# Graph attention kernel: the 0/1 matrix of destinations and the edge weights move into PSUM, and the two halves of a fetched set are masked by one VectorE operation

## The chip, the cores and the metric

The kernel runs on one core of one Trainium2 chip. The metric is the device time of one execution in microseconds (us). The engines are TensorE (PE, with its weight loads PEld), VectorE (DVE), ScalarE (ACT), GpSimd (POOL) and SyncE (SP, which here only issues transfers).

## What is computed

A graph attention layer with 4 heads is followed by a mixture of 16 experts, both on 6250 nodes with 256 features; the graph has 200,000 edges, sorted by destination. Cut to the graph part:

```
h_fwd, h_rev = h @ W_forward.T, h @ W_reverse.T          # 64 features each
messages = h_fwd[src] * direction[:, 0:1] + h_rev[src] * direction[:, 1:2]
scores = leaky_relu(einsum('ef,hf->eh', messages, attn_forward[0]), 0.2)
exp_scores = exp(scores - scores.max(axis=0))
norm = exp_scores / (segment_sum(exp_scores, dst, N)[dst] + 1e-10)
out = stack([segment_sum(messages * norm[:, hd:hd+1], dst, N) for hd in range(H)], axis=1)
```

The expert part (layer norm, gate, top 2 of 16 experts, two products each, layer norm) comes after it and is not touched by the change.

## The kernel before

A first stage makes a node table in DRAM. Each of its rows holds, for one node, 68 numbers of the forward weights (64 features and 4 score parts) and 68 of the reverse weights: 136 numbers. The edge stage, `stage_edges` from line 779 on, then goes through the edges in 98 chunks of 2048: 128 partitions by K = 16 sets of 128 edges. Two chunks are in the ring at a time (slots s = 0 and 1). The later stages (nodes, experts, final norm) take the last quarter of the time.

For one chunk c the work is:

- **GpSimd** (line 899) issues one indirect DMA per set (`gather`, line 262), which fetches the table rows of 128 source nodes into `rows`. The node numbers are offsets that the instruction reads from the tile `index` in SBUF. 14 of the 16 sets come this way; the last four chunks and the first two differ a little. Between the gathers stand waits on VectorE's messages (`msg_ready`), scores (`score_ready`) and TensorE's sums (`summed`) of the chunks before.
- **TensorE** (line 939) makes the other two sets (FILL = 2) by products instead of a fetch: `fetch` (line 959) multiplies a 0/1 matrix `onehot` by the table held in SBUF (`parts`), 28 products of 476 columns into `p_hot`, for 7 candidate places and for the two halves of the row (d = 0 and 1), each half in a PSUM bank of its own. It also sums the chunk's weighted messages into windows of nodes (line 878, `p_win`).
- **VectorE** (line 987) waits for all 16 sets, multiplies the rows by the edges' two weights (lines 990, 994 and 997, where the weights are read from `index` in SBUF), makes the 0/1 matrix `hot` of destinations (line 1003), adds the score parts (1009), applies the leaky part (1011), keeps the maximum (1016), adds the windows of the chunk before into the sums (985), adds forward and reverse parts into `msg` (1023), multiplies `hot` by the exponentials `ex` into `hot_ex` (1027), and, in `keep` (line 1049), masks the two fetched sets by place (1054, one operation for each half) and reduces them over the 7 places (1059). `build_hot` (1044) makes the next `onehot`.
- **ScalarE** takes the exponential (928), and **SyncE** loads `index` and `key` for the chunk after next (lines 888 and 892).

The order on each engine is the order in which the program is written; engines wait for each other by counting semaphores. The PSUM bank `p_dve` is VectorE's own and already holds `iota_p`, `rev_p` and `group_p`; the sum `p_part` is in PSUM too. All other operands of the lines above are in SBUF.

```
dve.tensor_tensor(rows[:, s, :, 0:COLS], rows[:, s, :, 0:COLS],
                  attr_of[:, 0, :].unsqueeze(2).broadcast_to([P, K, COLS]), ALU.mult)
```

Of the kernel before, what the change touches and what calls it, by code (L numbers as in the profile page):

```python
# [18 lines left out]
F32 = mybir.dt.float32  # L19
BF16 = mybir.dt.bfloat16  # L20
# [199 lines left out]
def stage_edges(nc, tensors, g):  # L220
# [4 lines left out]
    with ExitStack() as edges:  # L225
# [9 lines left out]
        before = esb("before", [1, NCH], I32)  # L235
        behind = esb("behind", [P, NU])
        place = esb("place_of_source", [P, NF])
        place_no = esb("place_no", [P, PLACES])
        key = esb("key", [P, RING, FILL, P])
        onehot = esb("onehot", [P, FILL, GP, P], F32R)  # L240
        group_first = esb("group_first", [P, GP])
# [25 lines left out]
        with ExitStack() as ctx:  # L267
# [128 lines left out]
            @block.gpsimd  # L396
            def _(pool):
                pool.memset(ident[:, :], 0.0).then_inc(s_init, 1)
                pool.wait_ge(s_init, 1)
                pool.affine_select(out=ident[:, :], in_=ident[:, :], compare_op=ALU.not_equal, fill=1.0,  # L400
                                   base=0, pattern=[[-1, P]], channel_multiplier=1).then_inc(s_ident, 1)
                pool.memset(ones[:, :], 1.0).then_inc(s_ident, 1)
                pool.iota(iota_w[:, :], pattern=[[1, W]], base=0, channel_multiplier=0,
                          allow_small_or_imprecise_dtypes=True).then_inc(s_ident, 1)
                pool.iota(place_no[:, :], pattern=[[GP * P, PLACES]], base=0, channel_multiplier=0,
                          allow_small_or_imprecise_dtypes=True).then_inc(s_ident, 1)
                pool.iota(group_first[:, :], pattern=[[P, GP]], base=0, channel_multiplier=1,
                          allow_small_or_imprecise_dtypes=True).then_inc(s_ident, 1)
                pool.memset(g["shared"][0:MSG, x_at + NT * D:HEADS * (NP + W)], 0.0).then_inc(s_init, 1)
                pool.wait_ge(s_hot, 32)  # L410
                def clear_x(i):

                    for copies, n in copied_part(i):
                        pool.wait_ge(copies, n)
                    pool.memset(x_rows[0:MSG, PARTS[i]:PARTS[i + 1], :], 0.0).then_inc(x_zeroed, 1)

                source = hot_key[0:NF // 3, :, :]
                late = hot_late[0:NF // 3, 0, :, :]
                rest, step = (spare[:, 6 * P + m * NF:6 * P + (m + 1) * NF] for m in range(2))
                pool.tensor_copy(source, source.bitcast(I32)).then_inc(s_init, 1)  # L420
                pool.tensor_copy(rest, place[:, :].bitcast(I32)).then_inc(s_init, 1)
                n = 4
                pool.wait_ge(s_init, n)
                pool.tensor_copy(place[:, :], rest).then_inc(s_init, 1)
                for much in (4, 2, 1):
                    for of, by in ((source, late), (rest, step)):
                        pool.tensor_scalar(by, of, float(much * GP * P), float(much * GP * P), ALU.is_ge, ALU.mult)\
                            .then_inc(s_init, 1)
                    n += 2 + (much == 4)
                    pool.wait_ge(s_init, n)  # L430
                    for of, by in ((source, late), (rest, step)):
                        pool.tensor_tensor(of, of, by, ALU.subtract).then_inc(s_init, 1)
                    n += 2
                    pool.wait_ge(s_init, n)
                pool.tensor_tensor(place[:, :], place[:, :], rest, ALU.subtract).then_inc(s_init, 1)
                assert n + 1 == KEYED

                for i in range(LATE):
                    pool.wait_ge(s_part, i + 1)
                    pool.tensor_tensor(part_of_parts(i, 1), tab[:, i % 4, 0:PARTS[i + 1] - PARTS[i], :],  # L440
                                       part_of_parts(i, 0).bitcast(F32), ALU.subtract).then_inc(s_init, 1)
                    clear_x(i)
                for i in range(LATE, NPART):
                    clear_x(i)

                for v in range(4):
                    pool.wait_ge(s_stored[v], 16 * ((NPART + 3 - v) // 4))
                pool.wait_ge(s_max, 2 * NPART)
                pool.wait_ge(s_init, parts_done)
                pool.wait_ge(s_low, low_late)  # L450
                for s in range(RING):
                    pool.wait_ge(index_ready[s], 16)
                    gather(pool, s, range(KG, K), early_rows)
                for s in range(EARLY + 1):
                    gather(pool, s, range(KG if s < EARLY else EARLY_SETS), gathered[s])
# [323 lines left out]
        with ExitStack() as ctx:  # L779
            sb, ps, sem = tensors(ctx)  # L780
            msg = sb("msg", [P, K, MSG])
            hot = sb("hot", [P, K, W], BF16)
            hot_ex = sb("hot_ex", [P, K, HEADS, W])
            raw = sb("raw", [P, K, HEADS])
            score = sb("score", [P, K, HEADS])
# [1 line left out]
            iota_x = sb("iota_x", [P, W])  # L787
            p_part = ps("p_part", [P, K, HD])
            p_win = ps("p_win", [P, 512])
            p_hot = ps("p_hot", [P, FILL, 2, 512])  # L790
            ex = sb("ex", [P, K, HEADS])
            p_dve = ps("p_dve", [P, 512])
            iota_p = p_dve[:, 0:W]
            rev_p = p_dve[:, W:W + K * HEADS].rearrange("p (k h) -> p k h", k=K)
            group_p = p_dve[:, W + K * HEADS:W + K * HEADS + GP]
            p_x = p_dve[:, 512 - HEADS * W:512]

            turns = sem("pool_turns")
            rev_part = sem("reverse_part_ready")
            fwd_part = sem("forward_part_ready")  # L800
            rev_score = sem("reverse_scores_ready")
# [42 lines left out]
            def all_rows(eng, c, s, it):  # L844

                eng.wait_ge(gathered[s], arrived(c, it))
                if isinstance(it, int) and it == 0:
                    eng.wait_ge(early_rows, 16 * HOT)
                elif not whole(it):
                    eng.wait_ge(hot_kept, 2 * (fill_of(s, it) + FILL))  # L850
# [32 lines left out]
            @block.sync  # L883
            def _(sp):
                def step(c, s, it, _):
                    if not whole(it):
                        sp.wait_ge(hot_built, FILL * (c - 1))
                        sp.dma_start(key[:, s, :, :], keys[ds(c * FILL, FILL), :].partition_broadcast(P))\
                          .then_inc(key_ready[s], 16)
                    after(sp, gathered[s], 16 * KG * it)  # L890
                    sp.wait_ge(rev_score, c - RING + 1)
                    sp.dma_start(index[:, s, :, :], edge[c] if isinstance(c, int)
                                 else edge[ds(c, 1)].rearrange("a p m k -> (a p) m k")).then_inc(index_ready[s], 16)

                sp.wait_ge(early_rows, 16 * HOT)
                chunks(sp, lambda it: None, step, RING)
# [38 lines left out]
            def _(pe):  # L935
# [23 lines left out]
                def fetch(f, s, it, j):  # L959

                    after(pe, hot_kept, 2 * (f - FILL + 1))
                    pe.wait_ge(hot_built, HOT + f + 1)
                    for gr in range(GP):
                        for m in range(2):
                            for d in range(2):
                                last = pe.matmul(p_hot[:, j, d, 0:PLACES * COLS], onehot[:, j, gr, :],  # L966
                                                 parts[:, gr:NT:GP, m, d * COLS:(d + 1) * COLS],
                                                 start=(gr == 0 and m == 0), stop=(gr == GP - 1 and m == 1))
                    last.then_inc(hot_rows, 1)
# [5 lines left out]
            def _(dve):  # L975
# [9 lines left out]
                    return dve.tensor_tensor(to, to, psum.rearrange("p (h w) -> p h w", h=HEADS), ALU.add)  # L985

                def step(c, s, it, loaded):
                    all_rows(dve, c, s, it)
                    attr_of = index[:, s, 1:3, :].bitcast(F32)
                    dve.tensor_tensor(rows[:, s, :, 0:COLS], rows[:, s, :, 0:COLS],  # L990
                                      attr_of[:, 0, :].unsqueeze(2).broadcast_to([P, K, COLS]), ALU.mult)\
                       .then_inc(fwd_part, 1)
# [56 lines left out]
                def keep(f, s, it, j):  # L1049

                    dve.wait_ge(hot_rows, f + 1)
                    found = p_hot[:, j, :, 0:PLACES * COLS].rearrange("p d (v c) -> p d v c", v=PLACES)
                    for d in range(2):
                        last = dve.scalar_tensor_tensor(  # L1054
                            out=found[:, d], in0=place_no[:, :].unsqueeze(2).broadcast_to([P, PLACES, COLS]),
                            scalar=place[:, ds(f, 1)], in1=found[:, d], op0=ALU.is_equal, op1=ALU.mult)
                    last.then_inc(hot_kept, 1)
                    dve.wait_ge(hot_kept, 2 * f + 1)
                    dve.tensor_reduce(rows[:, s, KG + j, :].rearrange("p (d c) -> p d c", d=2),  # L1059
                                      found.rearrange("p d v c -> p d c v"), AX.X, ALU.add).then_inc(hot_kept, 1)  # L1060

                def finish(c):

# [1133 lines left out]
```

## Time and profile before

| | |
|---|---|
| median of 3 runs | 2537.11 us (2532.44 to 2537.75) |
| the profiled execution, its own time | 2544.06 us |
| its span | 2542.3 us |
| POOL, PE, PEld, DVE, ACT busy | 67%, 79%, 69%, 73%, 14% |
| edge stage, first to last gather | about 62 to 1881 us of the span |

The profile is of one execution, on the only core. A busy share is an average over stages; which engine sets the pace of the edge stage has to be read from who waits for whom there. The time of a group of instructions can hold time in which the instruction stood still, if the engine had started it: a mean that lies above the shortest ones is a sign of that. "Idle before" is what an engine spent before a group, with what ended that time.

### The profile page before, as it was taken

What the parts mean: (1) busy time and instruction counts of PE and PEld (TensorE: products, weight loads), DVE (VectorE), ACT (ScalarE), POOL (GpSimd) and SP (SyncE); (2) the same over time, 40 slices, a digit from 0 to 9 for tenths busy, and PEclk for the clock granted to TensorE, in tenths of its full rate; (3) what the DMA queues carried; (4) which work ended last, traced back from release to release, by engine and by line L of the source; (5) the groups of instructions that cost most, each with busy time, mean ns of one, the idle gap of its engine ahead of it and who ended that gap; (6) DMA issues with size and microseconds to landing.
All of it is one profiled execution on the core that took longest, in us unless ns stands there. A gap on an engine that the chain in (4) does not pass through costs nothing.

```text
span 2542.3 us, 44100 instructions
## 1 busy us (share of the span) xinstructions
PE 2020.8 (79%) x11977; PEld 1765.1 (69%) x11978; DVE 1854.4 (73%) x4481; ACT 349.5 (14%) x936; POOL 1709.5 (67%) x1757
## 2 busy tenths in 40 slices
PE   7688888887888888788888888888727579999970
PEld 6577777676777777667777777777626568888870
DVE  6777777877777787777778777777747866666657
ACT  4100000000000000000000000000015524444435
POOL 6777777777777777777777777777745753333327
PEclk9699999999999899999999999999955589999995
DMA  6222222222222222222222222222244676655657
GB/s 203 61 63 59 64 59 64 61 59 63 59 64 58 63 61 59 63 59 64 58 64 61 59 64 59 64 58 64 57 135 131 211 228 199 196 196 197 198 167 270
DMA packets 176304, 256.65 MB, mean 101 GB/s; under 512 B 47078, under 2 KB 120999, under 8 KB 176004
## 3 DMA queue, kind: packets, MB, share of 16 engines
q0 software_dynamic: 53696, 121.60, 19.5%
q1 hardware_dynamic: 122564, 134.56, 17.3%
q8 instruction: 16, 0.26, 0.0%
q14 instruction: 28, 0.23, 0.0%
HBM read 218.11 MB, written 38.79 MB: 101 GB/s over the span
## 4 chain that ended last, share of the span: by engine, by line
POOL 42%; issue 25%; DVE 15%; PE 6%; DVEq 5%; DMA 5%; ACT 1%; SPq 0%; POOLq 0%; ACTq 0%
POOL rows L262 42%; DVEq L1704 3%; DMA rows<-node_table,index 2%; PE p_y L1872 1%; DVE p_y L1927 1%; PE p_h L1862 1%; DVE shared L985 1%; PE p_win L878 1%; DVE second L1907 1%; DVE hid_t L1899 1%; DVE p_part L994 1%; DVE back L1912 1%; DMA out<-shared 1%; DVE msg L1023 1%; DMA shared<-in_x 1%
## 5 line engine op out<-in xcount | busy, mean ns | idle before, releaser
L262 POOL DMA_INDIRECT rows<-node_table,index x1375 | 1378.3, 1002 | 443.8 <-issue 423.7
L966 PE MATMUL p_hot<-parts,onehot 128*128 128x476 f32 x5264 | 1193.4, 387 | 9.4 <-DVE rows L1059 5.1
L966 PEld LDWEIGHTS p_hot<-parts,onehot 128*128 128x128 f32 x5264 | 1003.7, 192 | 169.7 <-issue 14.4
L878 PE MATMUL p_win<-hot_ex,msg 128*65 128x64 f32 x3136 | 282.3, 268 | 334.4 <-DVE hot_ex L1027 333.3
L878 PEld LDWEIGHTS p_win<-hot_ex,msg 128*65 128x65 f32 x3136 | 267.5, 182 | 372.4 <-issue 372.4
L990 DVE TENSOR_TENSOR rows<-rows,index 128x1088 f32<-128x1088 f32 x98 | 126.7, 1292 | 333.0 <-DMA rows<-node_table,index 332.0
L1713 POOL DMA_INDIRECT expert_rows<-ys,back x104 | 103.0, 990 | 270.9 <-DVE ys L1932 199.0
L928 ACT ACTIVATE ex<-score,neg_shift 128x64 f32<-128x64 f32 x98 | 34.2, 349 | 1758.0 <-DVE score L1011 1758.0
L1054 DVE SCALAR_TENSOR_TENSOR p_hot<-place_no,place_of_source,p_hot 128x476 f32<-128x476 f32 x376 | 249.9, 709 | 0.0
L985 DVE TENSOR_TENSOR shared<-shared,p_win 65x64 f32 x784 | 170.3, 217 | 97.0 <-PE p_win L878 4.0
L1059 DVE TENSOR_REDUCE rows<-p_hot 128x136 f32<-128x952 f32 x188 | 216.1, 1150 | 6.5
L1862 PEld LDWEIGHTS p_h<-xt,shared 128*128 128x128 f32 x1664 | 199.9, 194 | 30.2 <-ACT xt L1804 27.5
L1862 PE MATMUL p_h<-xt,shared 128*128 128x128 f32 x1664 | 211.9, 281 | 7.2 <-ACT xt L1804 7.1
L1044 DVE TENSOR_TENSOR onehot<-key,p_dve 128x896 fp32r<-128x896 f32 x188 | 202.9, 1079 | 0.0
L1872 PE MATMUL p_y<-shared,hid_t 128*128 x832 | 198.7, 382 | 2.6 <-DVE hid_t L1899 2.2
L1872 PEld LDWEIGHTS p_y<-shared,hid_t 128*128 128x128 f32 x832 | 151.1, 192 | 19.7 <-issue 3.2
L1899 DVE TENSOR_SCALAR hid_t<-p_h,shared 128x128 f32<-128x128 f32 x208 | 63.4, 346 | 118.7 <-PE p_y L1872 79.5
L1283 POOL DMA_INDIRECT dispatched<-xn,slot_i x98 | 99.9, 1019 | 57.7 <-issue 35.2
L994 DVE TENSOR_TENSOR p_part<-rows,index 128x1024 f32<-128x1024 f32 x98 | 120.1, 1226 | 0.0
L1027 DVE TENSOR_TENSOR hot_ex<-hot,ex 128x1024 f32<-128x1024 bf16 x98 | 119.1, 1215 | 0.0
L1023 DVE TENSOR_TENSOR msg<-rows,p_part 128x1024 f32<-128x1024 f32 x98 | 118.5, 1209 | 0.0
L1835 ACT ACTIVATE own<-xs,is_first 128x256 f32<-128x256 f32 x104 | 52.9, 508 | 199.4 <-DVE is_first L1910 199.3
(268 smaller groups left out, 1408.2 us busy)
## 6 DMA issues: line engine op xcount, KB each, us to landing
shared<-in_w SPq DMA_DIRECT2D x120, 512.0 KB, 4.5
rows<-node_table,index POOLq DMA_INDIRECT x1375, 2.8
xs<-dispatched SPq DMA_DIRECT2D x104, 129.5 KB, 4.1
key<-hot_keys SPq DMA_DIRECT2D x94, 128.0 KB, 3.0
shared<-expert_rows SPq DMA_DIRECT2D x12, 896.0 KB, 7.8
token_rows<-in_x SPq DMA_DIRECT2D x7, 896.0 KB, 13.1
shared<-in_x SPq DMA_DIRECT2D x7, 768.0 KB, 9.0
out<-shared SPq DMA_DIRECT2D x6, 896.0 KB, 7.5
```

The costliest lines, as they stand in the source:

```text
L262: pool.indirect_dma_start(out=rows[:, s, k, :], out_offset=None, in_=table, in_offset=bass.IndirectOffsetOnAxis(ap=index[:, s, 0, k:k + 1] ...
L878: last = pe.matmul(psum[0:MSG, u * HEADS * W:(u + 1) * HEADS * W], msg[:, k, :], weighted[:, k, :, :].rearrange("p h w -> p (h w)"), start ...
L966: last = pe.matmul(p_hot[:, j, d, 0:PLACES * COLS], onehot[:, j, gr, :], parts[:, gr:NT:GP, m, d * COLS:(d + 1) * COLS], start=(gr == 0 an ...
L985: return dve.tensor_tensor(to, to, psum.rearrange("p (h w) -> p h w", h=HEADS), ALU.add)
L990: dve.tensor_tensor(rows[:, s, :, 0:COLS], rows[:, s, :, 0:COLS], attr_of[:, 0, :].unsqueeze(2).broadcast_to([P, K, COLS]), ALU.mult)\
L994: dve.tensor_tensor(p_part[:, :, :], rows[:, s, :, COLS:COLS + HD], attr_of[:, 1, :].unsqueeze(2).broadcast_to([P, K, HD]), ALU.mult)\
L1023: dve.tensor_tensor(msg[:, :, 0:HD], rows[:, s, :, 0:HD], p_part[:, :, :], ALU.add)\
L1044: dve.tensor_tensor(onehot[:, j, :, :], key[:, s, j, :].unsqueeze(1).broadcast_to([P, GP, P]), group_p.unsqueeze(2).broadcast_to([P, GP, P ...
L1054: last = dve.scalar_tensor_tensor(out=found[:, d], in0=place_no[:, :].unsqueeze(2).broadcast_to([P, PLACES, COLS]), scalar=place[:, ds(f, ...
L1059: dve.tensor_reduce(rows[:, s, KG + j, :].rearrange("p (d c) -> p d c", d=2), found.rearrange("p d v c -> p d c v"), AX.X, ALU.add).then_i ...
L1862: last = pe.matmul(p_h[:, u, f // 2, (f % 2) * P:(f % 2 + 1) * P], w1_r[:, r % R5, c, f * P:(f + 1) * P], xt[:, u, c, :], start=(c == 0), ...
L1872: last = pe.matmul(p_y[:, u, 0:D], hid_t[:, u, c, :], w2_sb[:, ds(e, 1), c, :] .rearrange("p a d -> p (a d)"), start=(c == 0), stop=(c == ...
```

## The change

`hot` becomes part of the PSUM bank `p_dve`, in 32-bit floats and no longer bfloat16 in SBUF. A new VectorE copy brings the chunk's edge weights (128 x 32) from `index` into the same bank as `weight_p`, ahead of the wait for the gathered rows, and lines 990, 994 and 997 read them there. SyncE's load of `index` now waits for that copy and no longer for the reverse scores. In `p_hot` the two halves of a fetched set now end and begin at the border of two banks, so that they adjoin, and `place_no` is written twice over, so that one operation masks both.

```diff
-        place_no = esb("place_no", [P, PLACES])
+        place_no = esb("place_no", [P, 2 * PLACES])
...
-                pool.iota(place_no[:, :], pattern=[[GP * P, PLACES]], base=0, channel_multiplier=0,
+                pool.iota(place_no[:, :], pattern=[[0, 2], [GP * P, PLACES]], base=0, channel_multiplier=0,
...
-            hot = sb("hot", [P, K, W], BF16)
...
-            p_hot = ps("p_hot", [P, FILL, 2, 512])
+            p_hot = ps("p_hot", [P, FILL, 1024])
+            half = PLACES * COLS
+            hot_from = 512 - half
...
+            hot_at = W + K * HEADS + GP
+            weight_at = hot_at + K * W
+            assert weight_at + 2 * K <= 512 - HEADS * W
+            weight_p = p_dve[:, weight_at:weight_at + 2 * K].rearrange("p (d k) -> p d k", d=2)
+            hot = p_dve[:, hot_at:hot_at + K * W].rearrange("p (k w) -> p k w", k=K)
...
-                    sp.wait_ge(rev_score, c - RING + 1)
+                    sp.wait_ge(weights_copied, c - RING + 1)
                     sp.dma_start(index[:, s, :, :], edge[c] if isinstance(c, int)
...
-                                last = pe.matmul(p_hot[:, j, d, 0:PLACES * COLS], onehot[:, j, gr, :],
+                                last = pe.matmul(p_hot[:, j, hot_from + d * half:hot_from + (d + 1) * half], onehot[:, j, gr, :],
...
                 def step(c, s, it, loaded):
+                    dve.wait_ge(index_ready[s], 16 * (it + 1))
+                    after(dve, raw_ready, c)
+                    after(dve, rev_part, c)
+                    dve.tensor_copy(weight_p, index[:, s, 1:3, :].bitcast(F32)).then_inc(weights_copied, 1)
                     all_rows(dve, c, s, it)
-                    attr_of = index[:, s, 1:3, :].bitcast(F32)
+                    dve.wait_ge(weights_copied, c + 1)
+                    attr_of = weight_p
...
-                    found = p_hot[:, j, :, 0:PLACES * COLS].rearrange("p d (v c) -> p d v c", v=PLACES)
-                    for d in range(2):
-                        last = dve.scalar_tensor_tensor(
-                            out=found[:, d], in0=place_no[:, :].unsqueeze(2).broadcast_to([P, PLACES, COLS]),
-                            scalar=place[:, ds(f, 1)], in1=found[:, d], op0=ALU.is_equal, op1=ALU.mult)
-                    last.then_inc(hot_kept, 1)
+                    found = p_hot[:, j, hot_from:hot_from + 2 * half]
+                    both = found.rearrange("p (v c) -> p v c", c=COLS)
+                    dve.scalar_tensor_tensor(
+                        out=both, in0=place_no[:, :].unsqueeze(2).broadcast_to([P, 2 * PLACES, COLS]),
+                        scalar=place[:, ds(f, 1)], in1=both, op0=ALU.is_equal, op1=ALU.mult).then_inc(hot_kept, 1)
```

The two places where VectorE's order changes are in the body of the loop over chunks. The first is the start of a chunk. Before:

```order
L850 ISA [waits gathered0]
L990 TENSOR_TENSOR rows<-rows,index 128x16x68 [waits one_hot_rows_kept]
L994 TENSOR_TENSOR p_part<-rows,index 128x1024 [waits messages_ready]
L997 TENSOR_TENSOR p_dve<-rows,index 128x64
L1003 ISA [waits weighted_hot_ready]
L1003 TENSOR_TENSOR hot<-dst_rel,p_dve 128x256
```

And with the change (its lines are numbered by the new file: 1002, 1006, 1009 and 1015 are the old 990, 994, 997 and 1003):

```order
L998 COPY p_dve<-index 128x32 [waits reverse_part_ready,raw_scores_ready,index_ready0]
L853 ISA
L857 ISA [waits gathered0]
L1000 REGISTER_ALU [waits one_hot_rows_kept]
L1002 TENSOR_TENSOR rows<-rows,p_dve 128x16x68 [waits edge_weights_in_psum]
L1006 TENSOR_TENSOR p_part<-rows,p_dve 128x1024 [waits messages_ready]
L1009 TENSOR_TENSOR p_dve<-rows,p_dve 128x64
L1015 ISA [waits weighted_hot_ready]
L1015 TENSOR_TENSOR p_dve<-dst_rel,p_dve 128x256
```

One copy is added ahead of the wait for the gathers, and each operation keeps its place; what was read from `index` and written to `hot` now lies in `p_dve`. The second place is `keep`, on VectorE at the end of the chunk. Before:

```order
L1054 SCALAR_TENSOR_TENSOR p_hot<-place_no,place_of_source,p_hot 128x476 [waits one_hot_rows_summed]
L1054 SCALAR_TENSOR_TENSOR p_hot<-place_no,place_of_source,p_hot 128x476
L1059 TENSOR_REDUCE rows<-p_hot 128x136 [waits one_hot_rows_kept]
L1054 SCALAR_TENSOR_TENSOR p_hot<-place_no,place_of_source,p_hot 128x476 [waits one_hot_rows_summed]
L1054 SCALAR_TENSOR_TENSOR p_hot<-place_no,place_of_source,p_hot 128x476
```

And with the change:

```order
L1066 SCALAR_TENSOR_TENSOR p_hot<-place_no,place_of_source,p_hot 128x952 [waits one_hot_rows_summed]
L1070 TENSOR_REDUCE rows<-p_hot 128x136 [waits one_hot_rows_kept]
L1066 SCALAR_TENSOR_TENSOR p_hot<-place_no,place_of_source,p_hot 128x952 [waits one_hot_rows_summed]
L1070 TENSOR_REDUCE rows<-p_hot 128x136 [waits one_hot_rows_kept]
L1056 TENSOR_TENSOR onehot<-key,p_dve 128x896 [waits one_hot_rows_summed,keys_loaded1]
```

Two operations of 476 elements become one of 952, twice per chunk. GpSimd's and TensorE's instructions keep their number and order.

## Rows read from the trace of the kernel before

**Rows 1.** The page: span, and busy time of each engine.

```profile
span 2542.3 us, 44100 instructions
PE 2020.8 (79%) x11977; PEld 1765.1 (69%) x11978; DVE 1854.4 (73%) x4481; ACT 349.5 (14%) x936; POOL 1709.5 (67%) x1757
```

**Rows 2.** The page: the chain that ended last, shares by engine.

```profile
POOL 42%; issue 25%; DVE 15%; PE 6%; DVEq 5%; DMA 5%; ACT 1%; SPq 0%; POOLq 0%; ACTq 0%
```

**Rows 3.** The view of waits, 300 to 1700 us: total us, times, longest us.

```profile
POOL rows L262 <- issue: 325.2, 1006, 2.2
...
DVE rows L990 <- DMA rows<-node_table,index: 245.8, 76, 5.5
PE p_win L878 <- DVE hot_ex L1027: 228.6, 76, 6.0
```

**Rows 4.** Starts of chunks 3 and 93 on VectorE, from the timeline (start us, duration us).

```profile
142.27 1.29 DVE L990 TENSOR_TENSOR rows<-rows,index 128x1088 f32<-128x1088 f32 x1 [2.91 <-DMA rows<-node_table,index]
...
1809.56 1.29 DVE L990 TENSOR_TENSOR rows<-rows,index 128x1088 f32<-128x1088 f32 x1 [2.92 <-DMA rows<-node_table,index]
```

**Rows 5.** The page's groups: busy us, mean ns of one | idle before, its releaser.

```profile
L262 POOL DMA_INDIRECT rows<-node_table,index x1375 | 1378.3, 1002 | 443.8 <-issue 423.7
...
L990 DVE TENSOR_TENSOR rows<-rows,index 128x1088 f32<-128x1088 f32 x98 | 126.7, 1292 | 333.0 <-DMA rows<-node_table,index 332.0
...
L1054 DVE SCALAR_TENSOR_TENSOR p_hot<-place_no,place_of_source,p_hot 128x476 f32<-128x476 f32 x376 | 249.9, 709 | 0.0
...
L1044 DVE TENSOR_TENSOR onehot<-key,p_dve 128x896 fp32r<-128x896 f32 x188 | 202.9, 1079 | 0.0
...
L994 DVE TENSOR_TENSOR p_part<-rows,index 128x1024 f32<-128x1024 f32 x98 | 120.1, 1226 | 0.0
L1027 DVE TENSOR_TENSOR hot_ex<-hot,ex 128x1024 f32<-128x1024 bf16 x98 | 119.1, 1215 | 0.0
L1023 DVE TENSOR_TENSOR msg<-rows,p_part 128x1024 f32<-128x1024 f32 x98 | 118.5, 1209 | 0.0
```

**Rows 6.** Groups of instructions, 1855.6 to 1871.6 us only: the gathers.

```profile
L262 POOL DMA_INDIRECT rows<-node_table,index x13 | 12.3, 944 | 4.0 <-issue 4.0
```

**Rows 7.** The timeline, one chunk around 1010 to 1023 us, GpSimd and VectorE.

```profile
1010.68 0.95 POOL L262 DMA_INDIRECT rows<-node_table,index  x1 [0.30 <-issue]
...
1013.45 1.29 DVE L990 TENSOR_TENSOR rows<-rows,index 128x1088 f32<-128x1088 f32 x1 [3.04 <-DMA rows<-node_table,index]
1014.43 1.13 POOL L262 DMA_INDIRECT rows<-node_table,index  x1 [0.30 <-issue]
...
1016.51 0.22 DVE L1011 SCALAR_TENSOR_TENSOR score<-raw 128x64 f32<-128x64 f32 x1
...
1016.77 0.23 DVE L1016 TENSOR_TENSOR run_max<-run_max,score 128x64 f32<-128x64 f32 x1
...
1020.57 1.21 DVE L1023 TENSOR_TENSOR msg<-rows,p_part 128x1024 f32<-128x1024 f32 x1
1020.87 0.94 POOL L262 DMA_INDIRECT rows<-node_table,index  x1 [0.30 <-issue]
1021.70 1.22 DVE L1027 TENSOR_TENSOR hot_ex<-hot,ex 128x1024 f32<-128x1024 bf16 x1
1022.12 1.61 POOL L262 DMA_INDIRECT rows<-node_table,index  x1 [0.30 <-DVE msg L1023]
```

**Rows 8.** The timeline: first and last of 97 gathers begun inside L1027.

```profile
95.73 1.22 DVE L1027 TENSOR_TENSOR hot_ex<-hot,ex 128x1024 f32<-128x1024 bf16 x1
96.32 1.44 POOL L262 DMA_INDIRECT rows<-node_table,index  x1 [0.30 <-issue]
...
1880.14 1.21 POOL L262 DMA_INDIRECT rows<-node_table,index  x1 [0.30 <-issue]
```

**Rows 9.** The timeline: a VectorE copy from SBUF into PSUM, and a pair of masks.

```profile
88.89 0.18 DVE L1105 COPY p_dve<-iota_w 128x16 f32<-128x16 f32 x1
...
1004.48 1.33 DVE L1054 SCALAR_TENSOR_TENSOR p_hot<-place_no,place_of_source,p_hot 128x476 f32<-128x476 f32 x2
```

More of the change, by code:

```diff
@@ L796, in stage_edges @@
             p_x = p_dve[:, 512 - HEADS * W:512]
+            hot_at = W + K * HEADS + GP
[3 more added lines that the diff above has]
+            hot = p_dve[:, hot_at:hot_at + K * W].rearrange("p (k w) -> p k w", k=K)
             turns = sem("pool_turns")
+            weights_copied = sem("edge_weights_in_psum")
             rev_part = sem("reverse_part_ready")
@@ L1051, in keep @@
                     dve.wait_ge(hot_rows, f + 1)
-                    found = p_hot[:, j, :, 0:PLACES * COLS].rearrange("p d (v c) -> p d v c", v=PLACES)
-                    for d in range(2):
-                        last = dve.scalar_tensor_tensor(
-                            out=found[:, d], in0=place_no[:, :].unsqueeze(2).broadcast_to([P, PLACES, COLS]),
-                            scalar=place[:, ds(f, 1)], in1=found[:, d], op0=ALU.is_equal, op1=ALU.mult)
-                    last.then_inc(hot_kept, 1)
+                    found = p_hot[:, j, hot_from:hot_from + 2 * half]
[3 more added lines that the diff above has]
+                        scalar=place[:, ds(f, 1)], in1=both, op0=ALU.is_equal, op1=ALU.mult).then_inc(hot_kept, 1)
                     dve.wait_ge(hot_kept, 2 * f + 1)
                     dve.tensor_reduce(rows[:, s, KG + j, :].rearrange("p (d c) -> p d c", d=2),
-                                      found.rearrange("p d v c -> p d c v"), AX.X, ALU.add).then_inc(hot_kept, 1)
+                                      found.rearrange("p (d v c) -> p d c v", d=2, v=PLACES), AX.X, ALU.add).then_inc(hot_kept, 1)
                 def finish(c):
```

## The prediction, made before the changed kernel ran

> **What bounds the kernel now.** I read the page's totals first and then asked who waits. TensorE has the largest busy share [rows 1], but the chain that ended last lies mostly on GpSimd and in "issue" [rows 2]. In the 1400 us from the middle of the edge stage, VectorE stands idle 245.8 us before L990, once per chunk, until a gather's transfer has landed, and TensorE 228.6 us before L878, once per chunk, until VectorE's L1027 is done [rows 3]. That is 3.2 and 3.0 us per chunk of slack on both. GpSimd waits for nobody: its 0.30 us between two gathers is nearly the same everywhere and stands as "issue" [rows 5, 7]. So GpSimd's row of gathers sets the pace, VectorE follows it by a transfer's latency (the last gather of a chunk ends at 1011.63, L990 starts at 1013.45), TensorE follows VectorE. Every eighth chunk one gap of GpSimd is 2.2 us long, also "issue" [rows 3]; nothing in the change touches it, and I leave it. A chunk takes (1809.56 - 142.27) / 90 = 18.53 us [rows 4]. Whatever shortens a gather shortens the time; whatever shortens VectorE alone only adds to its 3 us.
>
> **Gathers are not all alike.** Where VectorE does nothing, a gather takes 944 ns (13 of them) [rows 6]. The mean of all 1375 is 1002 ns [rows 5]. The difference, 1378.3 - 1375 x 0.944 = 80.3 us, is time in which gathers stood still. The timeline shows where [rows 7]: the gather that begins at 1022.12, 0.42 us into L1027, takes 1.61 us; the one that begins at 1014.43, inside L990, takes 1.13; the one that begins at 1020.87, inside L1023, takes 0.94. L990, L994, L997 and L1027 have both inputs in SBUF; L1023 has one in SBUF and one in PSUM. Each long gather is longer by what is left of the VectorE operation less 0.13 us: L1027 ends at 1022.92, 0.80 after the gather's start, and 0.80 - 0.13 is the 0.67 that 1.61 has over 0.94.
>
> - *Weights in PSUM.* L990, L994 and L997 keep one input in SBUF. Their gathers should take 944 ns: -9.7 - 7.3 - 1.8 = -18.8 us.
> - *`hot` in PSUM.* L1027 keeps only `ex` in SBUF: -60.8 us. Both terms lie on GpSimd's row, which is the path, so they count in full.
> - *Operations with a PSUM input.* Does one cost VectorE more? L1023 (one input in PSUM) takes 1209 ns for 1024 elements, L994 and L1027 (none) 1226 and 1215 [rows 5]. I take 0. L1003 writes 32-bit elements into PSUM where it wrote 16-bit ones into SBUF; L994 writes 1024 such in 1226 ns, so again 0.
> - *The new copy.* 128 x 32 into PSUM; the copy of 128 x 16 took 0.18 us [rows 9], so about 0.2 us, from below 0.18, from above 0.23 (L1016, with two inputs of 64) [rows 7]. It stands ahead of the wait for the gathers, where VectorE is idle 3.2 us per chunk [rows 3], so 0 on the path. Its own waits are for the same engine's operations of the chunk before and for an index load made a chunk earlier, all over by then. If the cover were gone it would cost 98 x 0.2 = 20 us.
> - *One mask for two.* Two operations of 476 take 709 ns each, overlap a little, and are done after 1.33 us [rows 5, 9]. At L1044's and L1023's slope, (1209 - 1079) / 128 = 1.02 ns per element, one of 952 takes 709 + 476 x 1.02 = 1.19 us against 1.33 for the pair [rows 5, 9]. It gives VectorE 0.14 us, 0.28 per chunk, which pays for the copy; bounds 0 and 0.24. On the path it is 0, since VectorE waits in any case. That the operation runs across a bank border no row shows; at worst it is the pair's 1.33.
> - *SyncE's queue.* The index load can now go when the gathers of its slot have landed, sooner by L990 and L994, 2.5 us [rows 5], and by L997. It is needed a chunk later: 0.
> - *TensorE.* The same products into the same banks at another column: 0. Its slack goes from 3.0 to 2.2 us per chunk as the period shrinks by 0.8; it stays covered.
> - *What is late next.* VectorE's idle time goes from 3.2 to about 2.4 us per chunk, so GpSimd still leads. Two operations keep two SBUF inputs, L1011 and L1016, 0.22 and 0.23 us [rows 7]. As gathers come earlier, one may begin there. For the chunk shown: the last gather before ends at 1011.63; undelayed, the fifth after it begins at 1011.63 + 0.30 + 4 x 1.249 = 1016.93, inside L1016, which ends at 1017.00 [rows 7]. Only 0.07 us is left, under the 0.13 that cost nothing. I take 0; the bounds are 0 and 0.25 us per chunk, 24 us in 98.
>
> The sum: 2544.06 - 79.6 = 2464.5 for an execution like the profiled one. That one lies 7 us above the median of the three runs, 2537.11, so the median to expect is 2537.1 - 79.6 = 2457.5, put as **2458 us**, 3.1% less. A measurement of this kernel can tell about 0.2%, 5 us, from no change.
>
> The place where a rule weighs on this is what a PSUM input costs. The rows above say 0. The Trainium skill ("VectorE: DVE Perf Modes", section on the TRN2 errata) gives VectorE a fixed cost of 120 cycles with a PSUM source and 58 from SBUF to SBUF; an estimate from that page is 65 ns more for each of four operations. By it L1016 would end some 0.2 us later, a gather would lose about 0.15 us in it, and the sum would be some 2472. The trace disagrees with it, as L1023 and L1027 show.
>
> **The rivals.**
>
> - *A new meeting, 2458 to 2482.* L1011 and L1016 catch a gather in each chunk: up to 24 us of the 80 come back, 2482 at most, about 2475. For it: the margin above is 0.06 us. Against: the operations are short. Chance 0.12.
> - *Nothing on GpSimd, 2537.* Gathers are lengthened by something else at those moments, such as the writes of those operations, or the offsets are not what is held up. Then only VectorE's hidden 0.1 us per chunk changes, and the time stays within 5 us of 2537. Against: L1023 writes as much into SBUF as L1027 and lengthens nothing; L994 writes only to PSUM and does. Chance 0.04. The Trainium skill ("SBUF — State Buffer", "Who interferes with whom") infers that a tensor_tensor takes only the shared read interface and that descriptor generation needs the write interface; by that rule these gathers would never have been held and the gain would be 0. The same section says that a VectorE instruction with two SBUF inputs contends with a GpSimd instruction that reads SBUF, and the long gathers of this trace agree with that sentence.
> - *VectorE becomes the bound, 2561.* If a PSUM input read by repetition (the weights, `hot`) ran at half rate, L990, L994, L997 and L1027 would grow by 3200 x 1.02 ns = 3.3 us per chunk. Its own work per chunk is now 18.53 - 3.23 = 15.3 us; with 3.3 more, and 0.1 less for masks and copy, it is 18.5, and no idle time is left to take up GpSimd's long gap, 2.2 us in every eighth chunk or 0.27 in each. That makes 18.78 us a chunk, 0.25 more than now, and 2537 + 98 x 0.25 = 2561. It decides from 3.2 us per chunk on; below that the time is GpSimd's. Against: L1044 reads `group_p` from PSUM repeated 128 times over, at 1079 ns for 896 elements. Chance 0.03.
> - That the change does not do what it says can be ruled out by its order: the four operations read `p_dve`, and `hot` is written there.
>
> **How the numbers follow.** The forecast itself has 0.81. The range goes from the fastest run less the sum, 2532.4 - 79.6 = 2453, and 3 us for the spread of runs, so 2450, up to the end of the first rival, 2482. The two others, 0.07, lie outside. Faster by over 0.2%: 0.81 + 0.12 = 0.93; within 0.2%: 0.04; slower: 0.03.
>
> **What would show it.** In the profile after: the mean of L262 at 944 to 950 ns with 1375 of them; the period of chunks at 17.7 us; VectorE's idle time before its first product at about 2.4 us per chunk less the copy; four products within 20 ns of their time before; a mask of 1.2 us, 188 of them; no gather over 1 us inside the four. It is wrong if the mean of L262 stays over 980 ns, if VectorE's idle time vanishes, or if GpSimd's gaps grow from 0.30 us.

## The result and the profile after

| | before | after |
|---|---|---|
| median | 2535.86 us (4 runs, 2532.44 to 2537.75) | 2461.9 us (4 runs, 2460.26 to 2465.95) |
| ratio | 1 | 0.9712, 95% interval 0.9695 to 0.9729 |
| span of the profiled execution | 2542.3 us | 2460.3 us |

The kernel is 74 us faster where 79.6 was forecast; 2461.9 lies in the range of 2450 to 2482. The page of the changed kernel, for [rows 1] and [rows 2]:

```profile
span 2460.3 us, 44109 instructions
PE 2004.1 (81%) x11977; PEld 1745.8 (71%) x11978; DVE 1835.5 (75%) x4391; ACT 349.1 (14%) x936; POOL 1633.0 (66%) x1757
...
DVE 26%; issue 24%; POOL 22%; DMA 11%; PE 8%; DVEq 7%; ACT 1%; SPq 1%; POOLq 0%; ACTq 0%
```

GpSimd's busy time fell by 76.5 us and the span by 82.0. The chain is shared out in another way than before: it now passes through VectorE and a gather's landing more often. That alone would suggest that VectorE now sets the pace. The waits say that it does not. From 300 to 1650 us, in the view of waits:

```profile
POOL rows L262 <- issue: 298.2, 919, 2.2
...
DVE rows L1002 <- DMA rows<-node_table,index: 204.7, 77, 4.3
PE p_win L885 <- DVE hot_ex L1039: 185.1, 76, 4.7
```

VectorE still stands idle 204.7 / 77 = 2.66 us per chunk before its first product (3.2 before, [rows 3]), TensorE 2.4 us (3.0 before), and GpSimd's gap is still 0.30 us. The page's groups, which answer to [rows 5]:

```profile
L262 POOL DMA_INDIRECT rows<-node_table,index x1375 | 1300.8, 946 | 443.3 <-issue 387.5
...
L1002 DVE TENSOR_TENSOR rows<-rows,p_dve 128x1088 f32<-128x1088 f32 x98 | 126.2, 1288 | 273.2 <-DMA rows<-node_table,index 273.0
...
L1066 DVE SCALAR_TENSOR_TENSOR p_hot<-place_no,place_of_source,p_hot 128x952 f32<-128x952 f32 x188 | 226.2, 1203 | 0.0
...
L1006 DVE TENSOR_TENSOR p_part<-rows,p_dve 128x1024 f32<-128x1024 f32 x98 | 119.8, 1222 | 0.0
L1039 DVE TENSOR_TENSOR hot_ex<-p_dve,ex 128x1024 f32<-128x1024 f32 x98 | 119.0, 1214 | 0.0
```

The mean gather went from 1002 to 946 ns, 1378.3 to 1300.8 us in sum: 77.5 us less. VectorE's products did not change (1292 to 1288, 1226 to 1222, 1215 to 1214 ns). The timeline of one chunk shows gathers beginning inside three large products and ending on time. The last one is the telling one, with 0.79 us of the product left; the one in L1006 begins with 0.11 us left, where it would have lost nothing in SBUF either:

```profile
955.61 1.29 DVE L1002 TENSOR_TENSOR rows<-rows,p_dve 128x1088 f32<-128x1088 f32 x1 [2.40 <-DMA rows<-node_table,index]
956.67 0.95 POOL L262 DMA_INDIRECT rows<-node_table,index  x1 [0.31 <-issue]
956.82 1.22 DVE L1006 TENSOR_TENSOR p_part<-rows,p_dve 128x1024 f32<-128x1024 f32 x1
957.93 0.95 POOL L262 DMA_INDIRECT rows<-node_table,index  x1 [0.30 <-issue]
...
963.76 1.21 DVE L1039 TENSOR_TENSOR hot_ex<-p_dve,ex 128x1024 f32<-128x1024 f32 x1
964.18 0.95 POOL L262 DMA_INDIRECT rows<-node_table,index  x1 [0.30 <-DVE msg L1035]
```

In [rows 7] the gathers at these places took 1.13 and 1.61 us. Over the whole trace 96 gathers begin inside L1039, 79 inside L1002 and 28 inside L1006 with over 0.2 us of the product left, and none of these takes over 0.96 us. Chunks 3 and 93, as in [rows 4], now begin at 139.52 and 1734.92 us, 17.73 us per chunk.

```profile
139.52 1.29 DVE L1002 TENSOR_TENSOR rows<-rows,p_dve 128x1088 f32<-128x1088 f32 x1 [1.54 <-DMA rows<-node_table,index]
...
1734.92 1.29 DVE L1002 TENSOR_TENSOR rows<-rows,p_dve 128x1088 f32<-128x1088 f32 x1 [2.45 <-DMA rows<-node_table,index]
```

### The profile page after: what moved, and what is told of

Read it like the earlier page. It is cut to its first block, busy times and chain, and to the rows that moved or that the text cites. A ratio compares the mean times of both kernels' runs of the same rounds, so it can differ in the third digit from the quotient of the medians.

```text
span 2460.3 us, 44109 instructions
## 1 busy us (share of the span) xinstructions
PE 2004.1 (81%) x11977; PEld 1745.8 (71%) x11978; DVE 1835.5 (75%) x4391; ACT 349.1 (14%) x936; POOL 1633.0 (66%) x1757
## 4 chain that ended last, share of the span: by engine, by line
DVE 26%; issue 24%; POOL 22%; DMA 11%; PE 8%; DVEq 7%; ACT 1%; SPq 1%; POOLq 0%; ACTq 0%
POOL rows L262 21%; DMA rows<-node_table,index 8%; DVE shared L992 5%; DVE p_part L1006 4%; DVEq L1715 3%; PE p_win L885 3%; DVE msg L1035 2%; PE p_y L1883 1%; DVE p_y L1938 1%; PE p_h L1873 1%; DVEq L876 1%; DVEq L992 1%; DVE hot_ex L1039 1%; DVE second L1918 1%; DVE hid_t L1910 1%
## 5 line engine op out<-in xcount | busy, mean ns | idle before, releaser
L262 POOL DMA_INDIRECT rows<-node_table,index x1375 | 1300.8, 946 | 443.3 <-issue 387.5
L885 PE MATMUL p_win<-hot_ex,msg 128*65 128x64 f32 x3136 | 261.7, 256 | 278.4 <-DVE hot_ex L1039 276.0
L885 PEld LDWEIGHTS p_win<-hot_ex,msg 128*65 128x65 f32 x3136 | 247.3, 170 | 316.7 <-issue 316.7
L1002 DVE TENSOR_TENSOR rows<-rows,p_dve 128x1088 f32<-128x1088 f32 x98 | 126.2, 1288 | 273.2 <-DMA rows<-node_table,index 273.0
L992 DVE TENSOR_TENSOR shared<-shared,p_win 65x64 f32 x784 | 170.3, 217 | 96.8 <-PE p_win L885 3.6
L1066 DVE SCALAR_TENSOR_TENSOR p_hot<-place_no,place_of_source,p_hot 128x952 f32<-128x952 f32 x188 | 226.2, 1203 | 0.0
L1006 DVE TENSOR_TENSOR p_part<-rows,p_dve 128x1024 f32<-128x1024 f32 x98 | 119.8, 1222 | 0.0
L1039 DVE TENSOR_TENSOR hot_ex<-p_dve,ex 128x1024 f32<-128x1024 f32 x98 | 119.0, 1214 | 0.0
```

The costliest lines, as they stand in the source:

```text
L262: pool.indirect_dma_start(out=rows[:, s, k, :], out_offset=None, in_=table, in_offset=bass.IndirectOffsetOnAxis(ap=index[:, s, 0, k:k + 1] ...
L885: last = pe.matmul(psum[0:MSG, u * HEADS * W:(u + 1) * HEADS * W], msg[:, k, :], weighted[:, k, :, :].rearrange("p h w -> p (h w)"), start ...
L1006: dve.tensor_tensor(p_part[:, :, :], rows[:, s, :, COLS:COLS + HD], attr_of[:, 1, :].unsqueeze(2).broadcast_to([P, K, HD]), ALU.mult)\
L1039: dve.tensor_tensor(hot_ex[:, :, :, :], hot[:, :, :].unsqueeze(2).broadcast_to([P, K, HEADS, W]), ex[:, :, :].unsqueeze(3).broadcast_to([P ...
L1066: dve.scalar_tensor_tensor(out=both, in0=place_no[:, :].unsqueeze(2).broadcast_to([P, 2 * PLACES, COLS]), scalar=place[:, ds(f, 1)], in1=b ...
```

## The experiments

The theory: GpSimd's gathers set the pace of the edge stage, and a gather waits while VectorE reads two tensors from SBUF. Rivals: the gain has another source (the index load that goes earlier, the single mask); what holds a gather is a write, not the second read; VectorE's own time is on the path. Beside the first four experiments the kernel before had a median of 2539.4 us, beside the last four 2540.2, and in the series of the result 2535.9. Gains are taken against the kernel before of the same series. The changed kernel itself was timed in the series of the result alone, so a comparison with its 2461.9 us is good to some 4 us.

### Weights alone

```diff
--- before
+++ this run
+            weight_p = p_dve[:, weight_at:weight_at + 2 * K].rearrange("p (d k) -> p d k", d=2)
...
+                    dve.tensor_copy(weight_p, index[:, s, 1:3, :].bitcast(F32)).then_inc(weights_copied, 1)
...
-                    attr_of = index[:, s, 1:3, :].bitcast(F32)
+                    attr_of = weight_p
```

> The kernel before with only the edge weights moved to PSUM (copy, and SyncE's wait with it); hot stays in SBUF as bfloat16 and the mask stays in two. Theory (a gather waits while VectorE reads two SBUF tensors): only the gathers begun inside the first three products are freed, 18.8 us, so about 2517; the mean gather goes from 1002 to 988 ns and the gathers inside the product hot x ex still take 1.5 to 1.7 us. Since all gathers come at other moments, the loss inside that product may move by some 10 us either way. Rival (the gain came from the index load that goes earlier, or from anything but the held gathers): 2536, or the whole 74 us at once, 2462.

Measured: 2528.0 us, ratio 0.9955 (0.9943 to 0.9967), 11.4 us faster. That is 11 us above the 2517 that were expected, and 1 us beyond the 10 allowed. The groups of its page and its timeline:

```profile
L262 POOL DMA_INDIRECT rows<-node_table,index x1375 | 1365.4, 993 | 443.5 <-issue 389.5
```

```profile
1014.64 1.22 DVE L1037 TENSOR_TENSOR hot_ex<-hot,ex 128x1024 f32<-128x1024 bf16 x1
1014.94 1.73 POOL L262 DMA_INDIRECT rows<-node_table,index  x1 [0.30 <-DVE msg L1033]
```

Nothing is lost in the three first products any more, which is 18.8 us. But with the delays ahead of it gone, the gather that meets the product with `ex` begins 0.30 us after its start (0.42 in [rows 7]) and is held longer, 1.73 us against 1.61. Over the trace 96 gathers lose 67.0 us there, where 97 lost 60.8 [rows 8]. 18.8 less 6.2 is 12.6, and 11.4 is measured. The index load goes earlier here as in the full change and the time falls by no more than the gathers account for, so that rival is out as the source of the whole gain.

### `hot` alone

```diff
--- before
+++ this run
-            hot = sb("hot", [P, K, W], BF16)
...
+            hot_at = W + K * HEADS + GP
+            hot = p_dve[:, hot_at:hot_at + K * W].rearrange("p (k w) -> p k w", k=K)
```

> The kernel before with only hot moved to PSUM; the weights are read from index in SBUF and the mask stays in two. Theory: the gathers begun inside hot x ex are freed, 60.8 us, so about 2475; no gather begun in that product is longer than 0.95 us, and those begun in the first two products still lose 0.1 to 0.6 us. The new phases may change that loss by some 10 us either way. Rival (it was the write of hot_ex, not the second input in SBUF): 2536.

Measured: 2479.4 us, ratio 0.9761 (0.9748 to 0.9774), 60.0 us faster, 4 above the expected 2475.

```profile
L262 POOL DMA_INDIRECT rows<-node_table,index x1375 | 1317.8, 958 | 443.5 <-issue 419.4
...
L1028 DVE TENSOR_TENSOR hot_ex<-p_dve,ex 128x1024 f32<-128x1024 f32 x98 | 118.9, 1214 | 0.0
```

No gather is held in the product with `ex` any more (L1028 in this run's file), although it writes the same 128x1024 floats into SBUF: the write is not what held it. (`hot` also goes from 16 to 32 bits here; the spare products below, with 32-bit inputs alone, take that rival out.) What is left in the first three products is 10.2, 7.3 and 1.8 us, 19.3 in sum. The two moves alone give 11.4 + 60.0 = 71.4 us; both together give 77.2 (below), since the 6.2 us that the first gives back has no place to be lost in.

### The mask alone, and all but the mask

```diff
--- before
+++ this run
-            p_hot = ps("p_hot", [P, FILL, 2, 512])
+            p_hot = ps("p_hot", [P, FILL, 1024])
...
-                    for d in range(2):
-                        last = dve.scalar_tensor_tensor(
-                            out=found[:, d], in0=place_no[:, :].unsqueeze(2).broadcast_to([P, PLACES, COLS]),
-                            scalar=place[:, ds(f, 1)], in1=found[:, d], op0=ALU.is_equal, op1=ALU.mult)
-                    last.then_inc(hot_kept, 1)
+                    dve.scalar_tensor_tensor(
+                        out=both, in0=place_no[:, :].unsqueeze(2).broadcast_to([P, 2 * PLACES, COLS]),
+                        scalar=place[:, ds(f, 1)], in1=both, op0=ALU.is_equal, op1=ALU.mult).then_inc(hot_kept, 1)
```

> The kernel before with only the mask in one operation over two adjoining banks. Theory: VectorE has slack, so 0: 2536 within 5 us; the masks take 1.20 us in place of 1.33 for two, and VectorE's idle time before its first product grows by 0.25 us per chunk. Rival (VectorE's time is on the path at all): 98 x 0.26 = 25 us faster, 2511.

Measured: 2541.9 us, ratio 1.0012 (1.0003 to 1.0021), 2.5 us slower. The page:

```profile
L262 POOL DMA_INDIRECT rows<-node_table,index x1375 | 1378.8, 1003 | 443.4 <-issue 423.3
...
L1056 DVE SCALAR_TENSOR_TENSOR p_hot<-place_no,place_of_source,p_hot 128x952 f32<-128x952 f32 x188 | 226.4, 1204 | 0.0
...
L992 DVE TENSOR_TENSOR rows<-rows,index 128x1088 f32<-128x1088 f32 x98 | 126.7, 1293 | 356.2 <-DMA rows<-node_table,index 355.3
```

The mask takes 1204 ns for what took 1.33 us in two, and all that VectorE saves becomes idle time before L992: 355.3 us in place of 332.0 [rows 5], 0.24 per chunk. The gathers are those of before, to 0.5 us in sum. The 2.5 us are inside the bound of 5 us that was set for no change. The interval excludes none at all. The profiled execution can't show them, since it took 2537.56 us and was the fastest of the eleven; its first gather to its last take 1819.4 us, as in the kernel before, whose profiled execution took 2544.06 us. Where the 2.5 us lie stays open.

The other side is the changed kernel with two masks:

```diff
--- after
+++ this run
-            p_hot = ps("p_hot", [P, FILL, 1024])
+            p_hot = ps("p_hot", [P, FILL, 2, 512])
...
-                        out=both, in0=place_no[:, :].unsqueeze(2).broadcast_to([P, 2 * PLACES, COLS]),
+                    for d in range(2):
```

> The changed kernel with the mask put back into two operations, both moves to PSUM kept. Theory: as the changed kernel, 2462 within 5 us, with the mean gather at 946 ns and VectorE's idle time before its first product 0.25 us per chunk shorter. Rival (the mask gave a part of the gain): up to 25 us slower, 2487.

Measured: 2462.2 us, ratio 0.9697 (0.9685 to 0.971), 77.2 us faster than the kernel before and within 0.3 us of the changed kernel's 2461.9. In ratios to the kernel before of each series that is 0.9697 with two masks, 0.9712 with one, and 0.9694 in the run of the long gap below, which has one too. No gain of the mask is seen in either place.

### Spare products that read two SBUF tensors, or one

```diff
--- after
+++ this run
+                        dve.tensor_tensor(p_part[:, 0:9, :], msg[:, 0:9, 0:HD],
+                                          weight_p[:, 0, 0:9].unsqueeze(2).broadcast_to([P, 9, HD]), ALU.mult).then_inc(spare_done, 1)
+                        dve.wait_ge(spare_done, 2 * c - 1)
+                        dve.tensor_tensor(p_part[:, 0:16, :], msg[:, 0:16, 0:HD],
+                                          hot_ex[:, 0:16, :, :].rearrange("p k h w -> p k (h w)"), ALU.mult).then_inc(spare_done, 1)
```

> The changed kernel with two spare VectorE products per chunk, results unused, ahead of the wait for the gathers and inside VectorE's idle time (1.9 of some 2.5 us): first 128x576 with one input in SBUF, to set the moment, then 128x1024 with both inputs in SBUF (msg, hot_ex) and the result in PSUM. It adds work and leaves none out. Theory (two SBUF inputs hold a gather, whatever the result is written to): a gather begins some 0.2 us after the second product's start and is held for what is left less 0.13 us, about 0.8 us per chunk, so 2462 + 97 x 0.8 = 2540, at least 2500; one gather per chunk takes 1.6 to 1.9 us. Rival (what holds a gather is a write to SBUF, or the work on bfloat16): 2462.

In the second run `hot_ex` is replaced by `weight_p`, in PSUM; the rest is the same:

> As the run with two SBUF inputs, but the second spare product (128x1024) takes one input in SBUF (msg) and the other in PSUM (the weights, repeated), at the same moment and of the same length. Theory: no gather is held and the work fits into idle time, so 2462 within 5 us. Rival (any VectorE work at that moment delays the gathers, or VectorE has no slack there): as the other run, or up to 2462 + 97 x 1.9 = 2646.

Measured: 2497.8 us (2486.8 to 2504.3), ratio 0.982 (0.9796 to 0.9844), with two SBUF inputs; 2462.6 us, ratio 0.9694 (0.9678 to 0.971), with one, the same as the changed kernel. The difference in the same series is 35 us. The timeline with two SBUF inputs, in two successive chunks:

```profile
973.48 1.23 DVE L1007 TENSOR_TENSOR p_part<-msg,hot_ex 128x1024 f32<-128x1024 f32 x1
973.63 1.89 POOL L262 DMA_INDIRECT rows<-node_table,index  x1 [0.30 <-issue]
...
991.05 1.23 DVE L1007 TENSOR_TENSOR p_part<-msg,hot_ex 128x1024 f32<-128x1024 f32 x1
992.08 1.02 POOL L262 DMA_INDIRECT rows<-node_table,index  x1 [0.30 <-issue]
```

And with one SBUF input:

```profile
971.42 1.23 DVE L1007 TENSOR_TENSOR p_part<-msg,p_dve 128x1024 f32<-128x1024 f32 x1
971.45 0.95 POOL L262 DMA_INDIRECT rows<-node_table,index  x1 [0.30 <-issue]
```

A gather that begins 0.03 us into a product with one SBUF input takes 0.95 us. One that begins 0.15 us into a product of the same length with two takes 1.89, of which 0.95 is being held: what is left of the product, 1.08, less 0.13. Both products write the same PSUM tensor, so only the read is different. (The PSUM input is read by repetition and the SBUF one is not; L994 of the kernel before repeats an SBUF input and held gathers too, 7.3 us in all, so repetition isn't what frees them.) This is the cleanest evidence for the rule. The price is half of what I expected, and 2 us under the least of 2500. I had put a gather 0.2 us after the product's start in every chunk; in fact it does so in about every other chunk and, the chunk after, comes mostly near the product's end (1.02 us). 99 gathers lose 49.5 us together. Some 8 us of that come back, since the long gap in every eighth chunk shrinks (below). The remaining 41 us belong to the profiled execution, which took 2504.3 us, 42 above the changed kernel's 2462.0. Why the four executions lie 17 us apart is open.

Two gathers of the same run show where the holding starts:

```profile
1119.16 1.23 DVE L1007 TENSOR_TENSOR p_part<-msg,hot_ex 128x1024 f32<-128x1024 f32 x1
1119.21 1.99 POOL L262 DMA_INDIRECT rows<-node_table,index  x1 [0.30 <-issue]
...
1701.39 1.29 DVE L1007 TENSOR_TENSOR p_part<-msg,hot_ex 128x1024 f32<-128x1024 f32 x1
1701.41 0.95 POOL L262 DMA_INDIRECT rows<-node_table,index  x1 [0.30 <-issue]
```

The gather that begins 0.05 us into the product is held until near its end. The one that begins 0.02 us into it is not held, and the product takes 1.29 us in place of 1.23: here VectorE waits for the gather. Four gathers begin 6 to 43 ns into this product; all four take 0.95 us, and the product is longer by 38 to 78 ns, which is each time the gather's offset and 31 to 35 ns. From 52 ns on a gather is held, until 0.13 us before the end. So the two shut each other out, whichever is first, and a gather that is first does so only for about 33 ns from its start (an estimate from these four).

The Trainium skill ("SBUF — State Buffer", "Who interferes with whom") says that a VectorE instruction with two SBUF inputs contends with a GpSimd instruction that reads SBUF, and these two runs agree. The same section infers that tensor_tensor leaves descriptor generation alone. Taken for a whole indirect gather that does not hold: the measured 1.89 against 0.95 us decides. That it is the reading of the offsets that is held fits the 33 ns, but no run shows it by itself.

### VectorE beyond its slack

```diff
--- after
+++ this run
+                        dve.tensor_tensor(p_part[:, 0:16, :], msg[:, 0:16, 0:HD],
+                                          weight_p[:, 0, 0:16].unsqueeze(2).broadcast_to([P, 16, HD]), ALU.mult).then_inc(spare_done, 1)
```

This stands three times ahead of the wait for the gathers.

> The changed kernel with three spare VectorE products of 128x1024 per chunk with one SBUF input each, ahead of the wait for the gathers: about 3.55 us, more than the idle time of 2.66 us per chunk (204.7 us by 77). Theory (GpSimd leads by VectorE's idle time and no more): VectorE becomes the bound, 0.9 us per chunk and a little for waits, 97 x 0.9 = 87, so about 2550 to 2575; idle time before the first product falls to near 0 and GpSimd begins to wait for VectorE. Rival (VectorE had more slack, or gathers run further ahead): 2462 to 2480.

Measured: 2597.8 us, ratio 1.023 (1.0213 to 1.0247), 136 us above the changed kernel and 23 beyond the expected range of 2550 to 2575. Its view of waits from 300 to 1700 us:

```profile
POOL rows L262 <- issue: 311.3, 946, 3.1
...
POOL rows L262 <- DVE score L1037: 118.8, 67, 2.0
DVE rows L1016 <- DVE p_part L1010: 20.0, 73, 0.3
```

The mechanism is as expected: VectorE no longer waits for gathers, and GpSimd waits for VectorE's scores, 1.8 us at a time. The price was sized too low. A chunk takes 19.15 us: 15.07 of VectorE's other work (17.73 less 2.66), three products at 1.23 with 0.03 us of wait ahead of each, 3.79, and 0.27 us for the last of them to be seen by the next product: 19.13. My 0.9 us per chunk had counted 3.55 for the products and no waits.

### The long gap

```diff
--- after
+++ this run
                     settle(pool, turns)
+                    settle(pool, turns)
```

> The changed kernel with each of GpSimd's four increments of a semaphore nobody waits for (settle) done twice per chunk. It asks where the 2.1 us gap between two gathers in every eighth chunk comes from. If it goes with the number of such instructions (32 of them per gap), it comes in every fourth chunk, 24 gaps, and the time is 12 x 1.8 = 22 us longer, 2484. If it goes with the number of gathers (112 per gap), 12 gaps stay and the time is 2462, within 5 us.

Measured: 2462.0 us (2 runs). Still 12 gaps of 2.1 us, 112 gathers apart. They don't go with these increments. Whether they go with the gathers, or with something else that comes once per chunk, can't be told here: 112 gathers are 8 chunks in every run. In the changed kernel one looks like this:

```profile
917.32 0.95 POOL L262 DMA_INDIRECT rows<-node_table,index  x1 [0.30 <-issue]
920.39 0.95 POOL L262 DMA_INDIRECT rows<-node_table,index  x1 [2.13 <-issue]
```

12 x 1.8 = 22 us of the time lie in these gaps. What fills them stays open.

## Why the prediction was right

- **The bound.** "GpSimd's row of gathers sets the pace" holds, before and after. VectorE took 2.0 us more per chunk at no cost (0.76 and 1.23, the spare products with one SBUF input), and 3.8 us more made it the bound.
- **Held gathers, -79.6 us.** In the two profiles the first gather to the last (start to end) takes 1819.4 us before and 1741.3 after, 78.1 less. Of the 79.6 nothing is left in the four operations. (The "1095 others" of the prediction are 1096, which changes nothing.) The undisturbed gather takes 946 ns in the changed kernel and not 944, 2 us in all; the run with two masks has 944, and so has the run of the long gap, with one mask, so the mask is not the reason and the size of 2 us is that of one profile against another. The medians moved by 74 us in this series, and by 77 in the next to the run with two masks (2539.4 to 2462.2). The last 2 to 5 us are within the spread of the medians of before, 2535.9 to 2540.2. That spread lies behind the edge stage as far as the profiles show: after the last gather come 661.0 us in the kernel before and 654.6 in the run with the mask alone, with the same 1819.4 us ahead of it.
- **The parts, 18.8 and 60.8.** `hot` alone gave 60.0. The weights alone gave 11.4 rather than 18.8; a first product that ends a gather's delay moves the next one deeper into the product with `ex`. Taken one at a time the terms don't add up; taken together they do.
- **PSUM inputs and the 32-bit `hot`, 0.** The products are within 4 ns of before, and L1015, which writes `hot`, went from 0.41 to 0.42 us. The Trainium skill's fixed cost of a PSUM source ("VectorE: DVE Perf Modes", the TRN2 errata), 65 ns more by the estimate, is not seen in these tensor_tensor operations.
- **The copy, 0 on the path.** 0.19 us each, ahead of the wait and partly beside the end of the operation before.
- **What is left of VectorE's idle time.** "About 2.4 us less the copy", so 2.2, was too low: 2.66 is measured. The prediction left the mask's 0.24 out of this sign, and of the copy's 0.19 only some 0.07 is taken from the idle time (3.24 to 3.05 us in the run with the weights alone, while the chunk shrank by 0.12). Nothing in the time hangs on it, as GpSimd leads either way.
- **The mask, 0 on the path.** 1.20 us against the 1.19 estimated, 188 times, across the border of two banks. VectorE saved 0.24 us per chunk and waited 0.24 longer.
- **The new meeting with L1028 (the old L1016), 0.** It came, and cost nothing. In the changed kernel 42 gathers begin while L1028 runs, and in the kernel before none began while L1016 ran. At most 0.10 us of it are left then (0.07 forecast), under the 0.13 us that cost nothing, and none is longer than 0.96 us. The one with 0.10 us left:

```profile
1402.18 0.22 DVE L1028 TENSOR_TENSOR run_max<-run_max,score 128x64 f32<-128x64 f32 x1
1402.31 0.95 POOL L262 DMA_INDIRECT rows<-node_table,index  x1 [0.31 <-DVE score L1023]
```

The margin is 0.03 us. In the run of the long gap, which has the changed kernel's VectorE part, 71 gathers begin there, with up to 0.17 us left, and four of them take 0.97 to 0.99 us. The rival (0.12) was close in its timing, but it was priced at up to 24 us, and no run has lost even 1 us there.

## What to carry to other kernels

Where GpSimd issues indirect transfers in a row, look at the spread of their durations, not at their sum: a mean of 1002 ns over a floor of 944 was 80 us here. If the long ones begin inside VectorE operations with both inputs in SBUF, moving one input into PSUM frees them, even when the operation itself doesn't get faster. Such terms depend on when each gather begins within the chunk, so measure the moves together; and a VectorE saving is worth nothing while VectorE waits for the gathers.

## What the runs showed of the hardware that was not expected

- A gather begun within the last 0.13 us of a VectorE product with two SBUF inputs loses nothing; one begun earlier loses the rest of it less 0.13 (0.95 us for 1.08 left). The exception is the product's first 43 ns: there the gather goes ahead and the product is the one held, for at most 78 ns.
- A gather that already runs when such a product starts is not held: 85 run at the start of L990 in the kernel before, 82 of them with over 0.3 us to go, and none takes over 0.96 us. One of the 85 begins 8 ns ahead of L990, and there the product takes 1314 ns in place of 1292.
- Every 112th gather (every eighth chunk) is preceded by a gap of 2.1 us, with twice the semaphore increments too. With the spare products that hold gathers, the same 12 gaps are 1.1 to 1.4 us, but for the first and the last, and cost 13.7 us above the usual 0.30 and not 22, so the gap seems to have a part that runs while gathers are held; that was not tried further.
- TensorE's mean granted clock from 300 to 1650 us was 0.94 before and 0.95 after, both mostly at the upper of its levels, 2.4 GHz. It waits 2.4 us per chunk before L885 where it waited 3.0 before L878, and the mean product of that line went from 268 to 256 ns. It is off the path.
